# Shifted copies in the halos of SiLU and of the last convolution, and another order of the low parts

## The reference

```
x = x + lattice(gn(x))      # 4 x 4 cells of 3x3 convolutions 48 -> 48, ReLU
x = x + circular(gn(x))     # 3x3 convolution 16 -> 16, circular padding
x = x + kan(gn(x))          # for each channel: SiLU and 8 cubic B-spline bases, then a 3x3 convolution 9*16 -> 16
x = x + conv(gn(x))         # 3x3 convolution 16 -> 16, zero padding, bias
```

## Time and profile before

| | |
|---|---|
| median of three runs | 1241.7 us |
| the profiled execution, its span | 1234.36 us, 1232.6 us |
| TensorE matmul, weight load busy | 95%, 71% |
| VectorE, ScalarE, GpSimd busy | 61%, 55%, 32% |

### The profile page before, as it was taken

How to read it: one execution, slowest core, us unless ns; L and a number is a source line. 1 busy time by engine, 2 the same in 40 slices (tenths; PEclk the granted TensorE clock), 3 DMA queues, 4 the chain that set the end, 5 groups by cost and what they waited for, 6 DMA issues and landing times.

```text
span 1232.6 us, 14837 instructions
## 1 busy us (share of the span) xinstructions
PE 1175.6 (95%) x5066; PEld 870.2 (71%) x5066; DVE 756.3 (61%) x956; ACT 678.1 (55%) x740; POOL 395.9 (32%) x573
## 2 busy tenths in 40 slices
PE   4989999999999999989999999999999997999996
PEld 3656677666666677766666677777777776777775
DVE  6888952475556522246655562235665789999962
ACT  3777754454554444444544443433543699999931
POOL 4432233444602012502112212743233534313423
PEclk9999999999999999999999999999999999999998
DMA  8999998999999868899999996978789624675773
GB/s 211 255 227 267 285 277 234 204 184 231 191 194 212 214 182 211 220 179 210 217 188 178 209 248 182 269 217 219 203 204 191 113 43 74 108 119 104 129 129 67
DMA packets 108062, 234.16 MB, mean 190 GB/s; under 512 B 40260, under 2 KB 53396, under 8 KB 99604
## 3 DMA queue, kind: packets, MB, share of 16 engines
q1 hardware_dynamic: 84000, 181.25, 66.5%
q0 software_dynamic: 15808, 24.38, 10.5%
q10 hardware_dynamic: 8180, 27.60, 7.0%
HBM read 124.66 MB, written 85.19 MB: 170 GB/s over the span
## 4 chain that ended last, share of the span: by engine, by line
PE 68%; SPq 13%; DVE 10%; DMA 3%; issue 3%; ACT 3%; POOL 0%; DVEq 0%; ACTq 0%
PE PB L1904 56%; SPq L875 11%; PE PB L1872 11%; DMA S<-lattice 2%; DVE F L1590 2%; DVE F L1602 2%; DVE S L1721 1%; DVE S L1734 1%; ACT F L1258 1%; DVE S L1727 1%; DVE F L1714 1%; DMA X<-in_x 1%; SPq L861 1%; PE PB L1850 0%; PE PB L1948 0%
## 5 line engine op out<-in xcount | busy, mean ns | idle before, releaser
L1904 PE MATMUL PB<-F,WA 128*96 128x512 f32 (+1 forms) x3792 | 916.9, 403 | 25.3 <-ACT S L1269 10.9
L1904 PEld LDWEIGHTS PB<-F,WA 128*96 128x96 f32 (+1 forms) x3792 | 662.0, 175 | 272.0 <-issue 20.3
L1258 ACT ACTIVATE F<-S 128x2116 fp32r<-128x2116 f32 (+4 forms) x160 | 261.6, 1635 | 194.1 <-DMA S<-lattice 66.3
L1269 ACT ACTIVATE S<-PB,BIAS 96x512 f32<-96x512 f32 (+1 forms) x320 | 211.5, 683 | 284.3 <-PE PB L1904 278.2
L1590 DVE TENSOR_TENSOR F<-S,F 128x1089 fp32r<-128x1089 f32 (+2 forms) x80 | 121.4, 1517 | 169.5 <-ACT F L1258 168.7
L1592 DVE TENSOR_TENSOR F<-S,F 128x1058 fp32r<-128x1058 f32 x64 | 80.7, 1261 | 187.0 <-ACT F L1258 186.4
L1602 DVE CAST F<-F 64x528 fp32r<-64x528 f32 (+4 forms) x304 | 183.6, 653 | 3.5
L986 POOL DMA_DIRECT2D WA<-taps x76 | 58.1, 767 | 332.3 <-ACT S L1269 290.9
L1872 PE MATMUL PB<-F,WA 128*128 128x512 f32 x576 | 145.0, 408 | 7.6 <-DVE F L1714 7.6
L1872 PEld LDWEIGHTS PB<-F,WA 128*128 128x128 f32 x576 | 110.3, 193 | 36.4 <-issue 8.8
L1593 DVE TENSOR_TENSOR F<-S,F 64x1058 fp32r<-64x1058 f32 x64 | 79.7, 1246 | 0.0
(11 more groups left out here) (159 smaller groups left out, 707.7 us busy)
## 6 DMA issues: line engine op xcount, KB each, us to landing
S<-lattice SPq DMA_DIRECT2D x448, 66.1 KB, 4.9
lattice<-S SPq DMA_DIRECT2D x32, 817.5 KB, 5.8
S<-lattice SPq DMA_DIRECT2D x158, 136.1 KB, 3.3
S<-lattice SPq DMA_DIRECT2D x72, 272.5 KB, 5.2
lattice<-S SPq DMA_DIRECT2D x50, 272.5 KB, 4.0
lattice<-S ACTq DMA_DIRECT2D x48, 272.5 KB, 5.0
lattice<-S ACTq DMA_DIRECT2D x16, 817.5 KB, 6.6
S<-lattice SPq DMA_DIRECT2D x158, 70.1 KB, 3.2
```

What stands on the lines that cost most here:

```text
L1258: act.activation(piece_view(s, h, 0), raw_view(s, h), ACT.Copy).then_inc(hi_ready, 1)
L1269: act.activation(wide(to[:, at:at + TS])[:, :, 0:RX], pixels(RING_BANK[n % SLOTS_O][0:cell.rows, :]), ACT.Relu, bias=BIAS[0:cell.rows, k:k ...
L1904: last = nc.tensor.matmul(bank, WA[0:rows, first:first + cell.rows], wide(FZ[0:rows, i % SLOTS_F, base:base + TS])[:, :, 0:RX], start=j == ...
```

## The change

- The halo tiles of SiLU and of the last convolution get a second copy in their upper 64 rows, shifted by one column (`shifted_halos`, four more DMAs each). The weights of the two column shifts are stacked in 128 rows to match (`single_spread` for W3, `kan_spread`), and TensorE does three matmuls where it did six. SyncE issues the second copy; for the last convolution of the last three images ScalarE does.
- VectorE: `feature_lo(n)` stands right behind `basis(n)` and what belongs between; ScalarE's `feature_hi(n)` moves between the two squares of round n + 1. `l3_split_lo`, `last_update` and `tail` now come behind `basis`.
- From image 4 on SiLU's low part is GpSimd's.
- `l1_update` is split into `l1_add` and `l1_stats`, and the group means and tails of the circular convolution's end come later; 8 and 16 of the warming matmuls go. An activation of one column with SiLU is put in the lattice's last cell.

```diff
+        def shifted_halos(own, halo):
+            for side, y in enumerate((3, 0)):
+                for s in range(2):
+                    src = own[s * 4 * C + y * C:s * 4 * C + (y + 1) * C].bitcast(F32)
+                    first = 4 * C + side * HALO + s * C
+                    dst = halo[first:first + C].bitcast(F32)
+                    if side == 0:
+                        yield dst[:, :, RW - 1:TS - 1], src[:, :, 0:TS - RW]
+                    else:
+                        yield dst[:, :, 0:TS - RW - 1], src[:, :, RW + 1:TS]
...
                 for dst, src in image_halos(slot[:, 0], slot[:, 1]):
                     sp.dma_start(dst, src).then_inc(l3_halo[max(0, b - B + 3)], 16)
+                if b < B - 3:
+                    for dst, src in shifted_halos(slot[:, 0], slot[:, 1]):
+                        sp.dma_start(dst, src).then_inc(l3_halo[0], 16)
...
+                        for dst, src in shifted_halos(feature(BASES), halo_tile(PAIRS - 1)):
+                            sp.dma_start(dst, src).then_inc(halo_rows[KAN_SETS], 16)
...
+            def silu_low_part(b):
+                pool.wait_ge(silu_ready, b + 1)
+                pool.wait_ge(silu_hi, b + 1)
+                pool.tensor_tensor(FR[:, 2, 0, 1], SILU, FR[:, 2, 0, 0].bitcast(F32), ALU.subtract)\
+                    .then_inc(silu_lo, 1)
...
+            for b in range(2, B):
+                if b >= 4:
+                    silu_low_part(b)
+                    out_part(b - 4, out_dmas(b - 4))
+                norm_event(2, b - 2)
...
                     kan_image(0)
+                    act.activation(SILU[:, 0:1], NS[0][:, 0:1], ACT.Silu)
...
             feature_hi(0)
+            distances(1)
+            distance_powers(1)
             for n in range(ROUNDS):
                 b, g = divmod(n, KAN_SETS)
-                if n >= 4:
-                    feature_hi(n - 1)
...
-                if n + 1 < ROUNDS:
+                if 1 <= n < ROUNDS - 1:
                     distances(n + 1)
                     if n == 1:
                         feature_hi(1)
-                    distance_powers(n + 1, 2 if n == 2 else None)
+                    distance_powers(n + 1, n if n > 1 else None)
...
                 l3_rows(b)
+                slot = l3_slot(b)
+                act.wait_ge(l3_lo, b + 1)
+                for dst, src in shifted_halos(slot[:, 0], slot[:, 1]):
+                    act.dma_start(dst, src).then_inc(l3_halo[b - B + 3], 16)
...
             tail(0, B - 1)
-            l1_update(3)
+            l1_add(3)
             inner(0)
             outer(0)
             l1_split_lo(B - 2)
-            tail(1, 3)
             basis(0)
-            l1_update(4)
+            l1_add(4)
             l1_split_lo(B - 1)
+            l1_stats(3)
             feature_lo(0)
-            l1_update(5)
-            tail(1, 4)
+            l1_add(5)
             inner(1)
             outer(1)
             silu_low(0)
             basis(1)
-            l1_update(6)
+            l1_add(6)
+            l1_stats(4)
             feature_lo(1)
             inner(2)
             outer(2)
             basis(2)
-            l1_update(7)
-            tail(1, 5)
+            l1_add(7)
+            l1_stats(5)
+            feature_lo(2)
             for n in range(3, ROUNDS):
                 b, g = divmod(n, KAN_SETS)
                 inner(n)
                 outer(n)
-                feature_lo(n - 1)
                 if n in (3, 4):
-                    tail(1, n + 3)
-                if g == 1:
+                    tail(1, 2 * n - 3)
+                basis(n)
+                if n in (3, 4):
+                    l1_stats(n + 3)
+                if n in (4, 5):
+                    tail(1, n + 2)
+                if g == 0 and b >= 3:
+                    update(b - 2)
+                if g == 1 and b < 4:
                     silu_low(b)
                 if g == 1 and b >= 3:
                     l3_split_lo(b - 3)
                 if g == 1 and b >= 4:
                     last_update(b - 4)
-                basis(n)
-                if g == 0 and b >= 2:
-                    update(b - 2)
                 if g == 1 and b >= 2:
                     tail(2, b - 2)
-            feature_lo(ROUNDS - 1)
+                feature_lo(n)
+                if n == 3:
+                    tail(1, 4)
+                if n == 4:
+                    update(0)
...
-            keep_warm(PB[3], 24)
+            keep_warm(PB[3], 16)
...
-                         at_shift(halo_tile(t), P, dx)) for dx in range(2)]
+                         at_shift(halo_tile(t), P, dx)) for dx in range(2 if t < PAIRS - 1 else 1)]
...
-                if b == 0:
-                    group_means(1, 6)
-                    keep_warm(PB[3], 16)
+                if b < 2:
+                    group_means(1, (4, 6)[b])
```

More of the change, by code:

```diff
@@ L693, in single_spread @@
                     blocks = [(s * 4 * C + y * C, 0, 4 - y) for y in range(4)]
-                    blocks += [(side * HALO + s * C, 2, (5, 0)[side]) for side in range(2)]
+                    for side in range(2):
+                        row, first = side * HALO + s * C, (5, 0)[side]
+                        if to is W1:
+                            blocks.append((row, 2, first))
+                            continue
+                        for shift in range(2):
+                            dst = to[shift * 4 * C + row:shift * 4 * C + row + C, part, 2, :].bitcast(F32)
+                            x = s + 2 - 2 * shift
+                            yield (dst.rearrange("p (s f) -> p s f", s=2),
+                                   src[:, x:x + 2, first * C:(first + 4) * C])
                     for row, tile, first in blocks:
@@ L731, in kan_spread @@
                                 row, y = odd * 4 * C + side * HALO + s * C, 3 * side
+                                rows = slice(2 * side * C, (2 * side + 1) * C)
                                 yield (blocks(halo_weights(part, 0, 0), n)[row:row + C, :, y * C:(y + 1) * C],
-                                       src[2 * side * C:(2 * side + 1) * C, odd * 4 * PAIRS:(odd * PAIRS + n) * 4])
+                                       src[rows, odd * 4 * PAIRS:(odd * PAIRS + n) * 4])
+                                if odd:
+                                    last = blocks(halo_weights(part, PAIRS - 1, 0), 1)[row:row + C, 2:4]
+                                    yield last[:, :, y * C:(y + 1) * C], src[rows, 4 * PAIRS - 4:4 * PAIRS - 2]
         def share(n, b, parts):
@@ L1169, in _ @@
             pool.memset(NS3, 0.0).then_inc(edge_done, 1)
-            norm_event(1, 5)
-            norm_event(1, 6)
-            norm_event(1, 7)
+            for b in range(3, B):
+                norm_event(1, b)
             def out_part(b, dmas):
@@ L1613, in l1_split_lo, with l1_add, l1_stats @@
                 nc.vector.tensor_tensor(lo[:, RW:RW + TS], ns, hi[:, RW:RW + TS], ALU.subtract).then_inc(l1_lo, 1)
-            def l1_update(j):
+            def l1_add(j):
                 dve.wait_ge(l1_done, j + 1)
                 nc.vector.tensor_tensor(X[:, j], OUT_BANK[j % 2][:, :], X[:, j], ALU.add).then_inc(added[1], 1)
+            def l1_stats(j):
                 dve.wait_ge(added[1], j + 1)
@@ L1659, in _ @@
                     if b >= 5:
-                        l1_update(b - 5)
+                        l1_add(b - 5)
+                        l1_stats(b - 5)
                     if b >= 1:
@@ L2006, in l3_step @@
                     keep_warm(PB[5], 12)
-                pe.wait_ge(l3_halo[z], 4 * 16 * (b + 1 if z == 0 else 1))
-                halo_part(LAST_BANK[b % 2], W3, l3_slot(b)[:, 1]).then_inc(l3_done, 1)
+                pe.wait_ge(l3_halo[z], 8 * 16 * (b + 1 if z == 0 else 1))
+                products(LAST_BANK[b % 2], [((W3[:, 0, 2], W3[:, 1, 2]), at_shift(l3_slot(b)[:, 1], P, 0))],
+                         False, True).then_inc(l3_done, 1)
             def halo_steps(b, g):
@@ L2013, in halo_steps @@
                 if g == 1:
-                    pe.wait_ge(halo_rows[KAN_SETS], (b + 1) * 64)
+                    pe.wait_ge(halo_rows[KAN_SETS], (b + 1) * 128)
                     halo_step(bank, PAIRS - 1, False)
@@ L2033, in _ @@
                         halo_steps(b - 1, 0)
+                        if b == 2:
+                            group_means(1, 7)
+                        if b >= 3:
+                            group_means(2, b - 2)
                     pe.wait_ge(feat_hi, KAN_SETS * b + g + 1)
@@ L2040, in _ @@
                         if b < 2:
-                            group_means(1, (5, 7)[b])
+                            group_means(1, (3, 5)[b])
+                        if b == 2:
+                            group_means(2, 0)
                         if b:
```

8 lines of the change are left out of this document (1 added, 7 removed).

## The result

The changed kernel takes 1262.31 us (median of 4 runs, 1262.03 to 1269.81), the kernel before 1241.66 us beside it (1240.21 to 1246.8): ratio 1.0173, interval 1.0126 to 1.0221. It is slower, by 20.7 us where the prediction had 20.

What follows compares the result with a forecast made beforehand. SyncE's queue was taken as deciding. F(14) at 1191.5 plus 39.3 us gave 1230.8 against 1209.5; with 0.5 and 0.7 back, +20 us on 1241.7: about 1262 us, own range 1253 to 1270, 8 in 10 within 1238 to 1272.

Steps and rivals of the forecast that it cites:

- TensorE, 11.5 us if it remains the bound: TensorE's SiLU and last-convolution halos: 3 matmuls fewer each per image, 48 in all, worth 11.5 us.
- The loop, at least 23.85 us: ScalarE and in-order VectorE waiting on each other: 11.14 us plus 12.7 us per image, against 23.33 before.
- Rival 2: Halos land in time and only the loop of ScalarE and VectorE holds: +4 us, 1246 us; chance 0.15.
- SyncE's queue, 27.0 us from F(2b) to F(2b+2): Between ends of feature_hi (F) in successive even rounds: 9.96 + 5.1 + 10.0 + 1.9 = 27.0 us.
- SiLU's low part on GpSimd: GpSimd's operation beside VectorE, from image 4 on: taken as nothing, with 4.4 us kept for the range.
- the first term: From the end of feature_hi through l3_split_lo (9.80 us) to SyncE's first halo issue 0.16 us later: 9.96 us.
- The landing: Group 0's eight halos, from first issue until landed, with GpSimd's store beside them: 10.0 us.
- rival 3: VectorE stands still beside GpSimd's SiLU part, 1.46 us in each of three images: 1266 us; chance 0.07.
- The start, spent by F(8): Feature_hi ends about 1.2 us earlier in round 6, but in round 8 at 1110.5 against 1106.8 before.
- The end, 39.3 us from F(14) to the last spline product: After feature_hi(14) ends: SyncE's remaining halos, then 12 matmuls in 2.9 us: 39.3 us.
- the sum: Last spline product at 1230.8 against 1209.5, 21.3 us later; with 0.5 and 0.7 back, +20 us.
- What would show it: Signs: feature_hi(8, 10, 12, 14) idle behind DMA; 16 halos queued; TensorE group-0 gaps of 2 us and more; VectorE gaps.

## Why the prediction was right

**TensorE, 11.5 us if it remains the bound.** It does not: of 27.2 us it has work for 23.6. The kernels with the shifted halos in the old order show that they do not come back there either, as VectorE is full.

**The loop, at least 23.85 us.** Right as a second limit, half a microsecond short: with the queue out of the way the period is 24.4. Rival 2, in which this loop alone holds, had 4 us for it; the kernel with the groups issued first is 8.4 us longer than before in the spline part and 9.5 in the timed runs.

**SyncE's queue, 27.0 us from F(2b) to F(2b+2).** Measured 27.46, 27.15 and 27.17. The mechanism was as told: l3_split_lo late, eight halos, then the group's eight. Term by term, from F(10): 11.19 us to SyncE's first issue for 9.96, 5.17 for 5.1, 8.91 to feature_hi for 10.0, 1.88 for 1.9. Two terms were off and cancel. SiLU's low part on GpSimd was costed at nothing, and lengthened the basis beside it from 2.36 to 3.30 us, which is 0.94 of the 1.23 us that the first term was short; the rest are hand-overs between operations. The landing was costed at 10.0 us from the first issue, with the store beside it; it was 9.25, 8.91 and 8.96. So rival 3's mechanism was there, at 0.94 us an image and not 1.46, hidden in the sum by a landing that was quicker by as much. That the two cancel is luck.

**The start, spent by F(8).** From l1_add(3), F(1) comes at 25.4 us (25.0 worked out), F(6) at 85.7 (84.2), F(8) at 113.0 (111.1), F(14) at 194.8 (192.1). The errors add up slowly, of one sign.

**The end, 39.3 us from F(14) to the last spline product.** Measured 41.3. The last halos landed at 37.1 us, for 36.4; the other 1.3 us are TensorE's: the 12 matmuls took 4.2 us and not 2.9, at a lower clock behind their wait. In all, the last spline product comes 236.1 us behind l1_add(3) for 210.1 before, 26.0 us later where the sum had 21.3.

**What would show it.** Three signs came: the four idle feature_hi, the queue with its 16 halos, VectorE with gaps. One was told in the wrong place: TensorE's gap of 3.4 us an image in the steady part stands in front of the last convolution's halo products, which wait for the eight halos in the queue, not in front of group 0.

The median came out at 1262.3 for 1262. The profile has 25.2 us in the spline part for the 20 of the sum; the profiled execution is 7.5 us above the median, and what of that lies in the spline part can't be told from one profile. So the mechanism is borne out, but the terms sum up 5 us short of the profile, and that the medians agree within a microsecond is in part luck.

## What to carry to other kernels

When work is moved back on one engine, look at what an in-order queue has behind the wait for it: here a DMA queue held eight transfers that were ready, for one operand that they do not use, and three lines' order was worth 16.8 us in the profiles, 11 in the timed runs. Before matmuls are traded for DMAs, count the issues: 32 of them, at 0.63 us and more, made a full queue. And an engine's saved time is worth nothing while the next one has as much work: take a piece of that work away and see whether the saving appears.

## What the runs showed of the hardware

TensorE's clock falls behind its new waits. Stretches of the changed kernel, the first behind the gap of 5.8 us, the others behind one of 3.4 (the clock is the third number from the right):
```profile
1241.40:1245.70 4.30, 4.29 (x13) 3.42 (x14) 0.00 (x0) 0.00 (x0) 0.00 (x0) 0.67 0.70 146
1169.40:1172.00 2.60, 2.60 (x8) 2.01 (x7) 2.50 (x2) 0.43 (x1) 0.69 (x1) 0.50 0.89 165
1172.00:1176.00 4.00, 4.00 (x17) 3.22 (x16) 2.36 (x6) 0.70 (x1) 0.00 (x0) 0.93 0.80 149
1176.00:1179.40 3.40, 3.40 (x15) 2.66 (x15) 2.09 (x2) 3.40 (x3) 0.00 (x0) 1.00 0.67 102
```
Behind 3.4 us of idle time (second row) it stands at 0.50, the lower of its two levels (1.2 GHz), and in the row from 1176.00 it is at 1.00 again. So an image's 36 matmuls there take 10.17 us for the 8.6 of 0.239 each, and TensorE looks busier (23.62 us) than its work is.

GpSimd and VectorE took turns. In the rows of VectorE and GpSimd above, the low part starts at 1154.94, while outer runs, which takes its usual 2.35 us; it ends at 1158.30, 1.2 us after outer; and basis, begun at 1157.22, ends 2.2 us after that, as if it had started when GpSimd was done. So GpSimd's operation seems to have waited for outer and run ahead of basis, and its price, 0.94 us, is most of those 1.2 us. I had taken a slow inner beside a copy of GpSimd for a small mutual drag. The Trainium skill (SBUF — State Buffer, SBUF: two separate sides) has two such operations exclude each other for a whole instruction, and these rows agree with it.

The kernel with l3_split_lo ahead of outer bears this out. There the same GpSimd operation starts beside the short l3_split_lo and takes 1.70 us for 3.36:
```profile
1143.93 0.70 DVE L1731 TENSOR_TENSOR WA<-KAN,WA 128x528 fp32r<-128x528 f32 x1
1144.11 1.70 POOL L1185 TENSOR_TENSOR F<-KS,F 128x528 fp32r<-128x528 f32 x1 [9.24 <-ACT F L1453]
1144.55 3.47 DVE L1771 SCALAR_TENSOR_TENSOR S<-S 128x2112 f32<-128x2112 f32 x1
```
Again it ends 1.2 us after the VectorE operation during which it started (1145.81 and 1144.63), and again the one behind, here outer, ends 2.2 us after that, 3.47 us for its 2.35. So the operation itself took about 1.2 us in both, and the rest of its 3.36 us was waiting.
